# Mixing of the expert weights: paired hi/lo rows in 8 steps of 128 columns, three row buffers, transposes and loads in quarters

## What is computed

```python
x = jnp.transpose(hidden_states, (1, 0, 2))
h = jax.nn.relu(jnp.einsum('bsh,oh->bso', x, gW1) + gb1)
gate = jnp.einsum('bsh,eh->bse', h, gW2) + gb2
g = gate.mean(axis=1)
W1 = jnp.einsum('be,eoi->boi', g, eW1)
b1 = g @ eb1
W2 = jnp.einsum('be,eoi->boi', g, eW2)
b2 = g @ eb2
y = jax.nn.relu(jnp.einsum('bsi,boi->bso', x, W1) + b1[:, None, :])
y = jnp.einsum('bsi,boi->bso', y, W2) + b2[:, None, :]
```

## Time and profile before

| what | us |
|---|---|
| median of 3 runs | 2550.09 |
| the profiled execution, its own time | 2555.59 |
| its span in the trace | 2553.7 |
| end of the state-space part (all engines meet, L1084) | 2241.2 |
| first mix | 2247.07 |
| stages 0 to 3 (16 mixes) | 2247.07 to 2286.16 |
| stages 4 to 31, up to the start of the last mix | 2286.16 to 2535.43 |
| last mix to the end of the span | 2535.43 to 2553.7 |

### The profile page before, as it was taken

How to read it: one execution, slowest core, us unless ns; L and a number is a source line. 1 busy time by engine, 2 the same in 40 slices (tenths; PEclk the granted TensorE clock), 3 DMA queues, 4 the chain that set the end, 5 groups by cost and what they waited for, 6 DMA issues and landing times. The chain is left out here.

```text
span 2553.7 us, 59918 instructions
## 1 busy us (share of the span) xinstructions
PE 2412.1 (94%) x23604; PEld 1505.2 (59%) x23604; DVE 1738.1 (68%) x3191; ACT 1194.7 (47%) x2485; POOL 1828.2 (72%) x1639
## 2 busy tenths in 40 slices
PE   5999999999999999999999999999989688889998
PEld 3666666666666666666666666666554222456555
DVE  5766666666666666766666666766647899866775
ACT  3344444444444434443444444443336788645554
POOL 5878887878778787878778787878730588765552
PEclk9999999999999999999999999999999899999999
DMA  7899999999999998989999999989963200056664
GB/s 203 175 186 188 184 189 181 186 179 194 181 183 186 187 188 182 186 181 193 181 187 187 186 190 178 186 180 195 190 135 69 55 1 1 6 121 120 124 119 85
DMA packets 1151035, 397.63 MB, mean 156 GB/s; under 512 B 1069185, under 2 KB 1121089, under 8 KB 1150625
## 3 DMA queue, kind: packets, MB, share of 16 engines
q1 hardware_dynamic: 1150752, 393.79, 78.0%
HBM read 125.22 MB, written 4.19 MB: 51 GB/s over the span
## 5 line engine op out<-in xcount | busy, mean ns | idle before, releaser
L607 PE MATMUL psum<-yN,hT 128*128 128x384 f16 x3072 | 775.6, 327 | 12.5 <-DMA lT<-xT 8.1
L608 PE MATMUL psum<-yN,lT 128*128 128x192 f16 x3072 | 754.0, 246 | 0.0
L591 PE MATMUL psum<-yT,Q 128*128 128x512 f16 (+2 forms) x4096 | 745.4, 334 | 0.0
L591 PEld LDWEIGHTS psum<-yT,Q 128*128 128x128 f16 x4096 | 377.6, 97 | 375.1 <-issue 88.7
L897 DVE TENSOR_REDUCE mx<-psum 128x1 f32<-128x801 f32 (+1 forms) x512 | 499.9, 987 | 82.2 <-PE psum L591 73.3
L547 POOL TENSOR_TENSOR pl<-prob,ph 128x1601 f16<-128x1601 f32 x128 | 414.1, 3235 | 183.7 <-DVE ph L906 154.0
L547 POOL TENSOR_TENSOR xT<-xT 128x1601 f16<-128x1601 f32 x128 | 413.3, 3229 | 157.8 <-DVE xT L906 112.8
L770 ACT ACTIVATE xT<-psum,nb 128x1601 f32<-128x1601 f32 x128 | 204.5, 1597 | 498.1 <-DVE nb L899 493.7
L770 ACT ACTIVATE prob<-psum,nb 128x1601 f32<-128x1601 f32 x128 | 204.5, 1597 | 497.9 <-DVE nb L899 497.9
L607 PEld LDWEIGHTS psum<-yN,hT 128*128 128x128 f16 x3072 | 300.8, 98 | 205.8 <-issue 17.1
L906 DVE CAST xT<-xT 128x1601 f16<-128x1601 f32 x128 | 155.0, 1211 | 221.7 <-ACT xT L770 221.7
(11 more groups left out here) (206 smaller groups left out, 3451.7 us busy)
## 6 DMA issues: line engine op xcount, KB each, us to landing
stage<-in_ctxN SPq DMA_DIRECT2D x96, 384.0 KB
wnat<-in_WF SPq DMA_DIRECT2D x31, 512.0 KB, 4.9
stage<-in_ctxT SPq DMA_DIRECT2D x32, 400.5 KB
stage<-in_ctxT SPq DMA_DIRECT2D x64, 200.2 KB
stage<-in_ctxT SPq DMA_DIRECT2D x32, 400.0 KB
stage<-in_ctxT SPq DMA_DIRECT2D x64, 200.0 KB
OT<-Oh SPq DMA_TRANSPOSE x256, 3.0
stage<-in_ctxR SPq DMA_DIRECT2D x64, 48.8 KB
```

Of the source, the lines that this page charges most:

```text
L591: ins = pe.matmul(psS[:, lo:hi], Q[p % 2][:, q, b, tt * P:(tt + 1) * P], yT[b][:, y, lo:hi], start=False, stop=(n == 3))
L607: pe.matmul(psO[:, 0:2 * CTX], hT[G % 2][:, n, :], yN[b][:, n, :], start=(n == 0), stop=False)
L608: pe.matmul(psO[:, 0:CTX], lT[G % 2][:, n, :], yN[b][:, n, 0:CTX], start=False, stop=False)
```

## The change

Hi and lo halves now lie side by side in one row group: 32 partitions hold 8 experts times 2 weight columns times {hi, lo}. A bank gets 8 matmuls of 128 columns (4 parts of 128 columns, each times the high and the low half of the gate) where it had 6 of 256. POOL's cuts are 4 and 4 instructions of twice the size. A stage is turned by four transposes of 512 columns in place of two of 1024, and loaded by four loads of two experts each (128 KB) in place of one. There are three row buffers. In SP's loop transposes and loads alternate, each quarter waits for one more mix of the stage two before, and the load is that of the stage two ahead. All four quarters wait for the low cut.

`QUADS` has two quads behind each mix; the turns stand behind the quads of k = 2, 4, 6 (and the fourth at the start of the next half), and ACT's `keep_pre` in the odd k. The gate's part is gone: its instructions stand at the head of the part that mixes, and PE's first mix waits for them by semaphore. DVE clears the rows of the expert biases first, since these are now loaded with 16 partitions of each 32.

The diff, cut to its core:

```diff
-        self.rows_in = [sem(f"ff_rows_in{n}") for n in range(2)]
-        self.cols, self.wrow = ([half[:, 4096 + 2048 * i + 1024 * w:5120 + 2048 * i + 1024 * w] for w in range(2)]
-                                for i in range(2))
+        self.rows_in = [sem(f"ff_rows_in{n}") for n in range(3)]
+        self.cols = half[:, 4096:6144]
+        self.wrow = [half[:, 6144 + 512 * h:6656 + 512 * h] for h in range(4)]
 
 
 def halves_by_column(pool, nat, cols, st, room):
 
-    hi, lo = (v.rearrange("p (v h q e a) -> p h v q e a", v=4, h=2, q=4, e=E) for v in cols)
-    nat = nat.rearrange("p e (v q h a) -> p h v q e a", v=4, q=4, h=2)
-    for h in range(2):
-        for v in range(4):
-            ins = pool.tensor_copy(hi[:, h, v], nat[:, h, v])
+    v = cols.rearrange("p (h n w e a) -> p h w n e a", h=4, n=16, w=2, e=E)
+    nat = nat.rearrange("p e (n h a) -> p h n e a", h=4, a=2)
+    for h in range(4):
+        ins = pool.tensor_copy(v[:, h, 0], nat[:, h])
     ins.then_inc(room.hi_cut, 1)
     pool.wait_ge(room.hi_cut, st + 1)
-    for h in range(2):
-        for v in range(4):
-            ins = pool.tensor_tensor(lo[:, h, v], nat[:, h, v], hi[:, h, v], ALU.subtract)
+    for h in range(4):
+        ins = pool.tensor_tensor(v[:, h, 1], nat[:, h], v[:, h, 0], ALU.subtract)
     ins.then_inc(room.lo_cut, 1)
 
 
-def turn_halves(sp, cols, rows, st, room):
-    for made, col, row in zip((room.hi_cut, room.lo_cut), cols, rows):
-        sp.wait_ge(made, st + 1)
-        sp.dma_start_transpose(row.rearrange("p (u n) -> p u n", u=8), col).then_inc(room.rows_in[st % 2], 16)
+def turn_halves(sp, cols, rows, st, h, room):
+    if h == 0:
+        sp.wait_ge(room.lo_cut, st + 1)
+    sp.dma_start_transpose(rows[h].rearrange("p (u n) -> p u n", u=4), cols[:, 512 * h:512 * h + 512])\
+      .then_inc(room.rows_in[st % 3], 16)
...
-        cols = [room.cols, [sb(f"wcol_{w}", [P, 8 * P], F16)[:, :] for w in ("hi", "lo")]]
-        rows = [room.wrow, [sb(f"wrow_{w}", [P, 8 * P], F16)[:, :] for w in ("hi", "lo")]]
-        whi, wlo = ([r[w].rearrange("p (u n) -> p u n", u=8) for r in rows] for w in range(2))
+        cols = [room.cols, sb("wcol", [P, 16 * P], F16)[:, :]]
+        wrow1, wrow2 = sb("wrow1", [P, 16 * P], F16), sb("wrow2", [P, 8 * P], F16)
+        rows = [room.wrow, [wrow1[:, 512 * h:512 * h + 512] for h in range(4)],
+                [xT[:, k, B * T:].bitcast(F16) for k in range(2)] + [wrow2[:, 512 * h:512 * h + 512] for h in range(2)]]
+        tiles = [[v.rearrange("p (v n) -> p v n", v=4) for v in parts] for parts in rows]
         hT = room.hT
-        Gbd = [sb(f"Gbd{n}", [P, T, 4], F16) for n in range(2)]
+        Gbd = [sb(f"Gbd{n}", [P, T, 2], F16) for n in range(2)]
...
-        def load_natural(sp, st):
+        def load_natural(sp, st, i):
             ob, q = divmod(st, 4)
             if q < 2:
                 src = a["WF"][0:E, :, q * DFF + ob * P:q * DFF + ob * P + P].rearrange("e p n -> p e n")
             else:
                 src = a["WF"][E + ob].rearrange("p (e n) -> p e n", e=E)[:, :, (q - 2) * P:(q - 1) * P]
-            sp.dma_start(wnat[st % 2][:, :, :], src).then_inc(wnat_in[st % 2], 16)
+            es = slice(2 * i, 2 * i + 2)
+            sp.dma_start(wnat[st % 2][:, es, :], src[:, es, :]).then_inc(wnat_in[st % 2], 16)
 
         def split(pool, st):
-            pool.wait_ge(wnat_in[st % 2], 16 * ((st + 1) // 2))
+            pool.wait_ge(wnat_in[st % 2], 64 * ((st + 1) // 2))
             if st >= 2:
-                pool.wait_ge(room.rows_in[st % 2], 32 * (st // 2))
+                pool.wait_ge(room.rows_in[(st - 2) % 3], 64 * ((st - 2) // 3) + 64)
             halves_by_column(pool, wnat[st % 2][:, :, :], cols[st % 2], st, room)
...
-        with ExitStack() as cs:
-            sbs = tensor_in(cs)
-            gW2, gb2, hs = room.gW2, room.gb2, room.sums
-            g32 = sbs("g32", [P, T])
-            wide = sem("wide")
-
-            gW2w = W2[:, 2:4, 0:P]
-            block = cs.enter_context(nc.Block())
...
-        QUADS = [range(0), range(0, 2), range(2, 4), range(4, 6), range(6, 8), range(8, 10), range(10, 12), range(12, 16)]
+        QUADS = [range(2 * k, 2 * k + 2) for k in range(8)]
...
+            for st in (1, 2):
+                for i in range(4):
+                    load_natural(sp, st, i)
+            sp.wait_ge(eb_clear, 2)
+            for q in range(3):
+                sp.dma_start(eb1r[32 * q:32 * q + 16, :], a["eb1"][:, None, :].to_broadcast([E, 2, DFF])).then_inc(w_small, 16)
+                sp.dma_start(eb2r[32 * q:32 * q + 16, :], a["eb2"][:, None, :].to_broadcast([E, 2, C])).then_inc(w_small, 16)
             for st in range(1, NST):
-                if st + 1 < NST:
-                    if st >= 2:
-                        sp.wait_ge(room.lo_cut, st)
-                    load_natural(sp, st + 1)
-                if st >= 2:
-                    for m in mixed:
-                        sp.wait_ge(m, 4 * (st - 1))
-                turn_halves(sp, cols[st % 2], rows[st % 2], st, room)
+                for i in range(4):
+                    if st >= 2 and st + i > 2:
+                        for m in mixed:
+                            sp.wait_ge(m, 4 * (st - 2) + i)
+                    turn_halves(sp, cols[st % 2], rows[st % 3], st, i, room)
+                    if st + 2 < NST:
+                        load_natural(sp, st + 2, i)
...
+                if n == 0:
+                    pe.wait_ge(g_step, 7)
+                    pe.wait_ge(eb_done, 1)
                 if v == 0:
-                    pe.wait_ge(room.rows_in[st % 2], 32 * (st // 2) + 32)
-                steps = [(h, w, g) for h in range(2) for w, g in ((whi, 0), (whi, 1), (wlo, 0))]
+                    pe.wait_ge(room.rows_in[st % 3], 64 * (st // 3) + 64)
 
                 def step(i, pair):
-                    h, w, g = steps[i]
+                    h, g = divmod(i, 2)
                     for q in (2 * pair, 2 * pair + 1):
                         r = slice(32 * q, 32 * q + 32)
-                        ins = pe.matmul(bank(psum, q)[:, 256 * h:256 * h + 256], w[st % 2][r, 2 * v + h, :],
-                                        Gbd[g][r, :, :].rearrange("p t a -> p (t a)"),
-                                        start=(w is whi and g == 0), stop=(w is wlo))
-                    if i == 5:
+                        ins = pe.matmul(bank(psum, q)[:, P * h:P * h + P], tiles[st % 3][h][r, v, :],
+                                        Gbd[g][r, :, :].rearrange("p t a -> p (t a)"), start=(g == 0), stop=(g == 1))
+                    if i == 7:
...
-                        if k in (4, 6):
-                            turn(ob, k // 2 - 2)
                         for q in QUADS[k]:
                             apply1(ob, q)
+                        if k in (2, 4, 6):
+                            turn(ob, k // 2 - 1)
                     elif ob:
                         if k == 0:
-                            turn(ob - 1, 2)
                             turn(ob - 1, 3)
                         for q in QUADS[k]:
                             apply2(ob - 1, q)
...
-                        if k in (4, 6):
-                            keep_turned(ob, k // 2 - 2)
-                        if k in (2, 4, 6, 7):
-                            keep_pre(ob, min(k // 2 - 1, 2) + k // 7)
+                        if k in (2, 4, 6):
+                            keep_turned(ob, k // 2 - 1)
+                        if k % 2:
+                            keep_pre(ob, k // 2)
                     elif ob and k == 0:
-                        keep_turned(ob - 1, 2)
                         keep_turned(ob - 1, 3)
 
```

More of the change, by code:

```diff
@@ L1464, in _ @@
                 sp.dma_start(room.gb1, a["gb1"].rearrange("(k p) -> p k", p=P)).then_inc(gate_in, 16)
[L1465 to L1467 removed]
+                for q in range(8):
+                    sp.dma_start(room.gb2[16 * q:16 * q + 16, :],
+                                 a["gb2"].rearrange("(e o) -> e o", o=1)[:, None, :].to_broadcast([E, 2, 1])).then_inc(gate_in, 16)
             sp.dma_start(wnat0, a["WF"][0:E, :, 0:P].rearrange("e p n -> p e n")).then_inc(room.wnat_in, 16)
[L1469 removed]
+            sp.wait_ge(gate_in, 16 * 11)
             sp.wait_ge(ln.turned, 6)
[L1471 removed]
+            for h in range(4):
+                turn_halves(sp, room.cols, room.wrow, 0, h, room)
         @block.vector
@@ L1705, in experts @@
         eb2s = sb("eb2s", [P, C], F16)
-        first = sb("first", [P, 4])
+        own = sb("own", [P, 2])
+        by_row = W1[1][:, 0, 0:32]
+        first = sb("first", [P, 1])
         ghi = sb("ghi", [P, T], F16)
-        glo = sb("glo", [P, T], F16)
+        glo = W1[1][:, 1, 0:T // 2].bitcast(F16)
         wnat_in = [sem(f"wnat_in{n}") for n in range(2)]
         w_small = sem("ff_w_small")
-        eb_done = sem("eb_done")
+        eb_done, eb_clear = sem("eb_done"), sem("eb_clear")
         g_mm = sem("g_mm")
@@ L1784, in experts @@
```

(35 more changed lines are left out.)

46 lines of the change are left out of this document (5 added, 41 removed).

## The result

The changed kernel takes 2556.52 us (median of 13 runs, 2552.58 to 2561.28), the kernel before 2551.01 beside it (13 runs, 2549.41 to 2555.08): 1.002 of the time, 95% interval 1.0012 to 1.0028. The change made it 0.2% slower where I had said 2528. The profiled execution spans 2553.9 us, almost the 2553.7 of before. Its experts' part began 3.8 us earlier (all engines meet at 2237.4 instead of 2241.2; the code in front of it is the same but for four small loads) and took 316.5 us instead of 312.5, so the loss is in the experts.

What follows compares the result with a forecast made beforehand. No engine was full; alternating mixes and ACT copies were taken as the bound. Seven blocks at -21.7, the end -0.3 and start 0 gave -22: profiled 2533.6, median 2528 us; own range 2520 to 2538, whole range 2516 to 2549.

Steps and rivals of the forecast that it cites:

- Shorter mixing: On PE, 8 steps of 0.056 us make a mix 0.63 us, 0.21 less; two mixes fall from 4.23 to 3.82.
- B: Weight loads on PE set the step at 0.107 us, a mix 0.16 to 0.2 us longer: 2566 us; chance 9%.
- D: The mix doesn't get shorter, because PE is handed 64 instructions where it was 48: 2543 us; chance 7%.
- Apply2 halves: The four stages with apply2, where DVE's work just matches the new chain: 15.95 us, 1.6 less.
- Round k = 0: First mix of an apply2 half, now with a turn and two quads behind it: 2.3 us against 1.76.
- Apply1 halves: The four stages with apply1, where PE sets the rounds with turns: 16.9 us, 1.5 less.
- Feeding: SP's issues take 1.85 us a quarter, 7.4 per stage, and fit the new stage of 8.2 us.
- the loop: Load issue, landing and POOL's cut behind SP's quarters: about 14.5 us, within the two stages, 16.4, it has.
- Rival A: The feeding sets the stage, at 8.85 us: 4 us less over 28 stages, 2546 us; chance 14%.
- POOL's cuts: POOL's 4 + 4 instructions of twice the size take 4.9 us, bounds 2.5 to 5.1.
- The start: First mix 1.9 us earlier, but stage 1 waits for its weights: 0 taken, bounds -6 to +4 us.
- The end: One turn less behind the last mix, most of it behind the wait for `hpre`: -0.3 us, up to -0.6.

Runs made afterwards that it cites:

- e3: Changed kernel with 2 transposes of 1024 columns a stage (3 for the third buffer) in place of four of 512: 2537.6 us.
- e7: Changed kernel with the loads of the experts' weights left out from stage 6 on: 2537.5 us.
- e11: Changed kernel with the weight loads from stage 6 on issued by ScalarE instead of SP: 2537.0 us.
- e12: Changed kernel with both transposes of 1024 columns and the weight loads from stage 6 on issued by ScalarE: 2535.5 us.
- e1: Changed kernel with transposes of 1024 columns (3 issues for the third buffer) and one load of 512 KB a stage: 2551.7 us.

## Why the prediction was wrong

- **Shorter mixing: right.** Two mixes take 3.82 us (1.74 + 2.08), the number forecast, and the steps of a mix come 0.056 us apart, as in the earlier trace rows. Rivals B and D are out. What the Trainium skill says of a weight load (TensorE: Matmul & The Clock Gate, LDWEIGHTS; 107 ns for 128 columns) does not hold here: four such loads of different groups and their matmuls pass in 56 ns.
- **Apply2 halves: right** where they are fed: 15.9 to 16.0 in e3, e7, e11 and e12 for 15.95. Round k = 0 takes 2.15 to 2.4 for 2.3.
- **Apply1 halves: a term missing.** Turn rounds take 2.25 where nothing stalls (2.30 forecast) and the half 16.5, but 17.4 to 18.2 on average. The term is the wait put down to "issue", behind the instruction packets; before has no such stall over 0.3 us from stage 4 on.
- **Feeding: the step that failed.** "A quarter is 1.18 to 1.57, a load 0.4 to 0.59, gaps 0.09: 1.67 to 2.25, I take 1.85." It measured 2.28, just over the upper end of that range: 9.1 a stage against a mixing of 8.2. I took the pace of one pair, the 2.65 us for two transposes of the earlier trace rows. The 1.57 of the median 128 x 384 transpose stood in the same group; with it and the 0.66 that a load measured the sum is 2.3. So did the means of before: its 52 transposes from stage 4 on take 1.41 us, its 25 loads 0.77, with the gap 2.27. The sum of the loop was read low as well: by its own terms (6.9, a landing of 2.3 to 4.9, a cut of 4.9) it is 14.1 to 16.7 against 16.4. "So in the steady part nothing waits" fell with it. Rival A had the mechanism and what would show it (a DMA releaser at each stage's first mix, SP without waits, though the waits list hid the second), but I priced it at 8.85 through its loop, and gave it 14%. The loop was not the bound, since e11 keeps it; the queue alone was, and by the forecast's own stage it decides from 8.2 / 4 = 2.05 us a quarter on.
- **POOL's cuts**: 4.1 us for 4.9, below my value and inside the bounds. POOL waits for `wnat` (130 us from stage 4 to the last mix), so nothing hangs on it.
- **The start: 0 forecast, 2 lost.** From the meeting of the engines the first mix is 3.3 us away (3.9 forecast, 5.9 before), stage 1 is 18.5 (19.3), stage 4 is 47.1 (44.6 forecast; 45.0 before). With wide transposes it is 44.8 in e3 and 43.2 in e12, but 48.6 in e1, so that the slow quarters alone account for it is not shown.
- **The end**: 16.4 us behind the last mix for 18.3 before, better than the -0.3 forecast.

In sum, over stages 4 to the end of the mixes: 228 forecast, 252.99 measured; 18 to 23 of the 25 us come back when SP's queue is lightened in any of three ways (e3, e7, e11), and the 2 to 7 that remain are the apply1 halves. Those three kernels and e12, at 2535.5 to 2537.6, lie inside the forecast's own 2520 to 2538: the gain of the shorter mix was there to be had, and the feeding took it.
